# A gather kernel's expert loop: ScalarE's sums wait for the products themselves, coefficients and diagonals stand two half heads behind them

## The reference

```python
q = batchnorm(x @ w_q)                       # 2 x 8 heads of 128
sim = einsum('pbnhd,hkpd->pbnhk', q, keys)   # 2 x 8 x 128 scores a token
sx, ix = top_k(sim[0], 8); sy, iy = top_k(sim[1], 8)
scores, pk = top_k(sx[..., :, None] + sy[..., None, :], 8)
indices = take(ix * 128 + iy, pk)            # 8 heads x 8 experts a token
h = gelu(einsum('bnd,bnhkd->bnhk', x, down_embed[indices]))
h = softmax(scores) * h
out = einsum('bnhk,bnhkd->bnd', h, up_embed[indices])
return x + out
```

## Time and profile before

| | |
|---|---|
| median of 3 runs | 3230.07 us |
| lowest to highest | 3229.87 to 3230.78 us |
| the profiled execution, its own time | 3229.33 us |
| its span, first to last instruction | 3227.2 us |
| mean granted TensorE clock | 0.982 of full speed |
| gathered through GpSimd's queue | 1073.87 MB, 83.1% of 16 engines' span |
| HBM, read and written | 350 GB/s over the span |

### The profile page before, as it was taken

One profiled execution on the slowest core, in us unless ns is written; L12 is line 12 of the kernel. 1 busy time (PEld: TensorE's weight loads), 2 busy tenths in 40 slices (PEclk: granted clock), 3 DMA queues, 4 the chain that ended last, 5 costly groups with the idle time before them and its releaser, 6 DMA issues.

```text
span 3227.2 us, 36087 instructions
## 1 busy us (share of the span) xinstructions
PE 2857.5 (89%) x10310; PEld 1373.1 (43%) x10310; DVE 2407.8 (75%) x5220; ACT 1820.0 (56%) x5589; POOL 2141.3 (66%) x2224
## 2 busy tenths in 40 slices
PE   8999999898888888888888888889888888888877
PEld 6777767343333333333333333333333333333322
DVE  5888715887777777777777777777777777777765
ACT  3566502665565555655656555555656555655554
POOL 1555513777777777777777777777777777777773
PEclk9999999999999999999999999999999999999999
DMA  6222103999999999999999999999999999999996
GB/s 226 80 70 75 39 30 141 395 412 411 413 412 411 412 412 412 411 412 412 412 411 413 412 412 412 412 411 411 412 409 408 411 411 410 411 408 406 409 410 246
DMA packets 324861, 1133.07 MB, mean 351 GB/s; under 512 B 36331, under 2 KB 36971, under 8 KB 324024
## 3 DMA queue, kind: packets, MB, share of 16 engines
q0 software_dynamic: 294912, 1073.87, 83.1%
q1 hardware_dynamic: 29088, 56.41, 4.9%
q10 hardware_dynamic: 664, 0.50, 0.1%
HBM read 1113.87 MB, written 16.78 MB: 350 GB/s over the span
## 4 chain that ended last, share of the span: by engine, by line
DMA 40%; PE 16%; POOL 14%; issue 11%; DVE 4%; ACT 0%; POOLq 0%; ACTq 0%; DVEq 0%
DMA rows<-in_table,expert_idx 37%; POOL rows L785 13%; PE banks L1330 11%; PE banks L1309 3%; DMA expert_more_rows<-in_table,expert_idx 3%; POOL expert_more_rows L785 1%; PE banks L1244 1%; DVE expert_top_i L889 1%; DVE expert_diag L980 1%; DVE rows L966 0%; PE banks L1256 0%; DVE expert_top_s L881 0%; DVE expert_coef L972 0%; PE banks L1285 0%; DVE expert_best_i L912 0%
## 5 line engine op out<-in xcount | busy, mean ns | idle before, releaser
L785 POOL DMA_INDIRECT rows<-in_table,expert_idx x1824 | 1725.1, 946 | 658.0 <-issue 541.0
L1330 PE MATMUL banks<-rows,expert_diag 128*128 128x512 f32 x3648 | 1710.9, 614 | 307.3 <-DVE expert_diag L980 307.0
L1149 ACT ACTIVATE rows<-rows 128x512 f32<-128x512 f32 x1824 | 1124.3, 617 | 945.2 <-DVE expert_coef L972 942.8
L966 DVE TENSOR_TENSOR rows<-rows,banks 128x2048 f32<-128x2048 f32 x456 | 1043.0, 2287 | 543.0 <-DMA rows<-in_table,expert_idx 541.5
L1330 PEld LDWEIGHTS banks<-rows,expert_diag 128*128 128x128 f32 x3648 | 687.4, 194 | 1283.0 <-issue 752.8
L1309 PE MATMUL banks<-amat,expert_xnT 128*128 128x512 f32 x992 | 465.2, 592 | 2.0 <-ACT banks L1140 1.3
L980 DVE TENSOR_TENSOR expert_diag<-banks,expert_coef 128x512 f32<-128x512 f32 x512 | 348.2, 680 | 0.6
L1149 ACT ACTIVATION_READ_ACCUMULATOR rows<-rows 128x1 f32 x1824 | 339.9, 186 | 0.0
L1309 PEld LDWEIGHTS banks<-amat,expert_xnT 128*128 128x128 f32 x992 | 188.3, 190 | 238.8 <-issue 229.9
L785 POOL DMA_INDIRECT expert_more_rows<-in_table,expert_idx x224 | 212.7, 950 | 84.1 <-issue 73.9
L1330 PE MATMUL banks<-expert_more_rows,expert_diag 128*128 128x512 f32 x448 | 209.8, 612 | 39.1 <-DVE expert_diag L980 39.1
(11 more groups left out here) (125 smaller groups left out, 2087.8 us busy)
## 6 DMA issues: line engine op xcount, KB each, us to landing
rows<-in_table,expert_idx POOLq DMA_INDIRECT x1824, 14.6
attention_xT_t<-in_x_T SPq DMA_DIRECT2D x32, 256.0 KB, 3.1
attention_x_t<-in_x SPq DMA_DIRECT2D x32, 256.0 KB, 3.1
x_dram<-rows SPq DMA_DIRECT2D x32, 256.0 KB, 2.0
expert_x_t<-x_dram SPq DMA_DIRECT2D x32, 256.0 KB, 6.1
out_y<-expert_x_t SPq DMA_DIRECT2D x32, 256.0 KB, 6.1
rows<-in_w_q SPq DMA_DIRECT2D x4, 1024.0 KB, 6.1
rows<-in_w_qT SPq DMA_DIRECT2D x4, 1024.0 KB, 8.6
```

The costliest lines, as they stand in the source:

```text
L785: pool.indirect_dma_start(four(n)[:, k, :], None, table[:, :], bass.IndirectOffsetOnAxis(ap=idx[:, t % 2, at:at + 1], axis=0))\
L966: return dve.tensor_tensor(down, down, xn_ps[:, par, :].unsqueeze(1).to_broadcast([P, HALF, D]), ALU.mult)
L1149: ins = act.activation(down, down, ACT.Copy, accum_out=hid[:, j % RING, k:k + 1])
L1330: mm = pe.matmul(out_ps[:, par, :], diag[:, j % RING, k, :], four(t * HALVES + j)[:, k, D:2 * D], start=(j == 0 and k == 0), stop=(j == HA ...
```

## The change

VectorE now signals every `products` (`multiplied`), and ScalarE waits for that instead of for coefficients. The coefficients and diagonals in step j are those of half head j - 2 instead of j - 1; the two that are left over after the last tile stand behind the loop. TensorE's chunks 2 and 3 of the scores move from half heads 8 and 11 to 7 and 10, and the transposes from 14 to 13, since TensorE's matmuls now stand one VectorE step later. Chunks 0 and 1 stay. VectorE also waits, before the coefficients, for its own earlier products to be complete.

```diff
--- before.py
+++ after.py
@@ -992,15 +992,15 @@
                 for j in range(HALVES):
                     n = t * HALVES + j
                     dve.wait_ge(row_in[n % GROUPS], (n // GROUPS + 1) * 64)
-                    made_products = products(t, par, j)
-                    if first and j == 0:
-                        made_products.then_inc(ev["multiplied"], 1)
+                    products(t, par, j).then_inc(ev["multiplied"], 1)
+                    if n > 0:
+                        dve.wait_ge(ev["multiplied"], n)
                     if j in (4, 6, 11, 14) and more >= 2:
                         wait(dve, "scored", (t + 2) * NQ + (4, 6, 11, 14).index(j) + 1)
-                    if j > 0:
-                        coefficients(t, par, j - 1)
+                    if j > 1:
+                        coefficients(t, par, j - 2)
                     elif not first:
-                        coefficients(t - 1, 1 - par, HALVES - 1)
+                        coefficients(t - 1, 1 - par, HALVES - 2 + j)
                     if j == 0:
                         if more >= 1:
                             top_places(3)
@@ -1065,10 +1065,10 @@
                             weights(1 - par)
                         if more >= 2:
                             pair_places(0)
-                    if j > 0:
-                        diagonals(t, j - 1)
+                    if j > 1:
+                        diagonals(t, j - 2)
                     elif not first:
-                        diagonals(t - 1, HALVES - 1)
+                        diagonals(t - 1, HALVES - 2 + j)
 
             made = 0
 
@@ -1124,8 +1124,9 @@
             norm(2, 0, 1)
             wait(dve, "ident_kept", 1)
             run(step)
-            coefficients(NT - 1, 1, HALVES - 1)
-            diagonals(NT - 1, HALVES - 1)
+            for j in (HALVES - 2, HALVES - 1):
+                coefficients(NT - 1, 1, j)
+                diagonals(NT - 1, j)
             finish(NT - 1, 1, NT // 2 - 1)
 
         @block.scalar
@@ -1151,11 +1152,7 @@
 
             def step(t, par, half, more, first):
                 for j in range(HALVES):
-
-                    if first and j == 0:
-                        wait(act, "multiplied", 1)
-                    else:
-                        wait(act, "coef_done", t * HALVES + j)
+                    act.wait_ge(ev["multiplied"], t * HALVES + j + 1)
                     sums_of_products(t, j)
                     wait(act, "summed", t * HALVES + j + 1)
                     act.activation(act_h[:, j % RING, :], hid[:, j % RING, :], ACT.Gelu_apprx_tanh)\
@@ -1313,9 +1310,9 @@
                     mm.then_inc(ev["scored"], 1)
 
             def step(t, par, half, more, first):
-                chunk_at = {0: 0, 2: 1, 8: 2, 11: 3}
+                chunk_at = {0: 0, 2: 1, 7: 2, 10: 3}
                 for j in range(HALVES):
-                    if j == 14 and more >= 3:
+                    if j == 13 and more >= 3:
                         turn(t + 3)
                     if more >= 2:
                         for c in range(2):
```

## The result

The changed kernel takes 3237.14 us, the median of 14 runs (3235.16 to 3239.44), against 3230.06 us of 14 runs of the kernel before (3228.81 to 3232.06). The ratio is 1.0022, with a 95% interval of 1.0014 to 1.003: **7.1 us more, 0.22%**. The forecast was 3234.6 us, 4.5 us more, in a range of 3231.0 to 3238.5. The profiled execution took 3237.47 us.

The account below looks back on a forecast made before the run. The prediction took the DMA engines' gathers to bound the kernel. 1.1 us at the start plus 3.4 us at the end, 4.5 us on a median of 3230.07, gave 3234.6 us, in a range of 3231.0 to 3238.5.

Parts of the forecast that it names:

- The bound: Expert loop: DMA gathers set the pace, 5.09 us a half head; ScalarE's 945 us of idle time counted 0.
- Rival C: ScalarE's wait was a bound after all: 0.16 us off each half head, 3148 us, or a smaller part; chance 0.03.
- Coefficients and diagonals one step later in the middle: Middle of loop: slots freed some 5.1 us later, gathers' lead falls from 27.5 to about 22.4 us, cost 0.
- Rival B: Lead of 22.4 us too short for the DMA engines: each of 57 ring turns loses 1 us, 3287 us; chance 0.03.
- The prediction's own sign against itself: Middle of loop: DMA windows below 409 GB/s would mean the lead or the order of the scores matters after all.
- The added wait: VectorE's wait for its own products each half head: hidden in 1.2 us of idle time, counted 0.
- The start: Start of loop: first diagonals 1.6 us later, TensorE's first group partly at slow clock; 1.1 us, ends 0.5 and 2.9.
- two ways in which the clock could come back: TensorE's first group: as long after the first matmul as before, term 1.6 us; or at the same moment, 0.5 us.
- The end: After the last products: three groups of TensorE matmuls follow instead of two, last addition 3.43 us later.
- Scores half a head sooner: TensorE's score chunks and transposes: later steps in the first tile may be late, slots not; 0, at most 1.7 us.
- rival A: Start: slow clock through the first group and beyond, term from 3.0 up to 8 us, time 3238 us; chance 0.16.
- both terms and no other: Only the losses at loop start and end: 3233.5 to 3236.5 us, chance 0.68.

Follow-up runs that it names:

- e4_act: The kernel before, with only ScalarE's sums changed to wait for the products instead of the coefficients: 3230.96 us, ratio 1.0001.
- f2_nowait: The changed kernel without VectorE's added wait for its own products: 3234.16 us, ratio 1.0015 to the kernel before.
- e5_ring8: The kernel before with a ring of eight half heads for the gathers instead of nine: 3253.46 us, ratio 1.0073.
- f1_selfwait: e4_act plus VectorE's added wait for its own products, lag and score order as in the kernel before: 3232.11 us, ratio 1.0009.
- e1_tail: The changed kernel with coefficients and diagonals again one half head behind in the last tile: 3233.86 us, ratio 1.0011 to the kernel before.
- e2_start: The changed kernel with one half head of lag and the old score and transpose places in the first tile: 3237.11 us, ratio 1.0017 to the kernel before.
- e3_both: The changed kernel with one half head of lag in first and last tile, old score places in the first: 3232.69 us, ratio 1.0009 to the kernel before.
- g1_lean: The kernel before with VectorE's waits for up_done and scored moved to instructions without other waits, 609 instructions fewer: 3225.68 us, ratio 0.9989.
- g5_pairs: g1_lean with coefficients and diagonals made for two half heads at once from the second tile on: 3228.84 us, ratio 0.9994 to the kernel before.
- e7_warm: The changed kernel with seven extra TensorE matmuls while it waits for the first diagonals: 3234.84 us, ratio 1.0015 to the kernel before.

## Why the prediction was right or wrong

**The bound: right.** The gathers bound the loop before and after; ScalarE's 945 us of idle time were no bound, and e4_act shows the edit that gives the change its name at 0 within 1 us. Rival C is out.

**Coefficients and diagonals one step later in the middle, counted 0: right.** The lead fell to 23 to 24 us (forecast 22.4), and f2_nowait, with that lead, has the middle pieces of the kernel before. Rival B is out. Its trial by e5_ring8 changed more than the lead and proves nothing. The prediction's own sign against itself, a DMA window under 409 GB/s, did come up: 408 from 2000 to 2400 us. It was a false alarm. f1_selfwait has 411 GB/s in that window at the long lead and yet the same middle piece (2343.80 and 2343.58 us), and from 2800 to 3200 us the order is turned round, 402 GB/s in the kernel before and 409 in the changed one. The windows count what all DMA engines move, the pace is set by what lands last. The rows are f1_selfwait, then the kernel before, then the changed one:

```profile
2000.00:2400.00 400.00, 347.46 (x781) 146.08 (x780) 308.19 (x682) 236.64 (x724) 288.31 (x305) 0.98 1.03 411
```

```profile
2800.00:3200.00 400.00, 332.24 (x732) 135.95 (x730) 291.35 (x561) 231.57 (x720) 281.43 (x299) 0.98 1.01 402
```

```profile
2800.00:3200.00 400.00, 327.70 (x726) 133.36 (x724) 291.70 (x571) 231.48 (x720) 288.07 (x306) 0.99 1.02 409
```

GpSimd's waits for TensorE, which should have risen, are 86.5 us and not 84.3, so hardly:

```profile
  issue: 600.4, 1820
  PE banks L1327: 86.5, 109
```

That was a poor sign to name: once the ring is full, GpSimd waits as much at a lead of 24 us as at one of 28.

**The added wait, counted 0: wrong, and this is the step that failed.** I reasoned that VectorE has 1.2 us of idle time a half head to hide it, which is so, and looked only at VectorE's own time. The price lies elsewhere: it makes 390 instructions, all VectorE's, and each 128th instruction of VectorE comes with a fetch after which the gathers land 0.9 us late. f1_selfwait and f2_nowait put the wait at 1.2 to 3.0 us by their medians, and three long gaps more are 2.8. It is nearly all of the difference between 4.5 and 7.1 us.

**The start, taken at 1.1 us with ends of 0.5 and 2.9: the later first group was right, the clock's return was not as assumed, and the size is within the ends.** The profiled execution showed nearly the upper one: its first group had almost all passes at 1.2 GHz, 6.60 us. From the first products to the first release of a slot it is 15.60 us in the changed kernel, 14.27 in e1_tail and 14.76 in f2_nowait; with the old lag at the start it is 13.04, 13.98, 13.15, 14.16 and 13.42 us in before, e4_act, f1_selfwait, e2_start and e3_both. The means are 14.9 and 13.6, a term of 1.3 us; with g1_lean and g5_pairs (14.0 us each, old lag too) it is 1.2. Three executions against seven, each scattered by about 1 us, do not fix it better than that. The prediction had two ways in which the clock could come back, and neither holds: over these ten traces it returns 3.2 to 5.9 us after the start of the first group, and 11.3 to 14.9 us after the first products. The rule from the Trainium skill, "TensorE: Matmul & The Clock Gate", Part 1, that the moment of the clock's return does not follow the work, agrees with this scatter of about 1 us between kernels that are the same up to there. The prediction read it as a moment that stands, which would have made the term 0.5 us; the mean of the traces is nearer to the 1.6 of the shift alone. The clock's part can be had back: e7_warm gained 2.3 us.

**The end, 3.43 us: right,** to the hundredth in the trace, 3.3 us in the medians of e1_tail.

**Scores half a head sooner, counted 0: right.** VectorE waited in the first tile for chunk 0, which now comes a step later, 2.80 us ahead of the coefficients at 585.52 us, but no slot was late by it: half heads 9 to 21 are all issued 1.4 to 1.6 us later than before, by the clock of the span.

Of the rivals, A was forecast to decide beyond a first term of 3.0 us. That point was not passed in the mean (1.3 us); by its median the change is slower by over 0.2% for another reason, a third term that none of the rivals named. The sum as measured: 3.4 at the end, 1.3 at the start and 2.4 left for the instructions, 7.1 us; the 2.4 is what remains, and lies within the 1.2 to 3.0 us of the experiments.

**The range: right in part by luck.** To both terms and no other the forecast gave 3233.5 to 3236.5 us, and 3237.14 lies above that. It lies within 3231.0 to 3238.5 because the range was kept wide for rival A, a slow clock at the start; the room was filled by the fetched instructions.

## What to carry to other kernels

An idle engine's largest wait says nothing before it is known what the engine ahead of it waits for; here 945 us of it were worth nothing. When a kernel is bound by DMA, look for the moments at which the DMA engines run dry, at the start and the end of the loop, and price every edit there; in the middle look at what lands last, and whether long gaps come at a fixed count of some engine's instructions. Then the length of that engine's list has a price, waits included: a second wait ahead of an instruction was an instruction of its own here (f1_selfwait, 391 more), and moved to a neighbour that waited for nothing it was not (g1_lean, 609 fewer).

## What the runs showed of the hardware that was not expected

VectorE's instruction fetch makes gathers land late. Once in 128 of VectorE's instructions (127.8 to 128.0 in the mean of every trace looked at) the last of the 64 completions of a half head comes 0.9 us late, while the 60th does not. 100 instructions of VectorE more or less move the end by 0.5 to 0.8 us, in both directions. 450 fewer on GpSimd did not move the middle of the loop, and of the 8 KB packets that come at other counts of VectorE none lies in a long gap. Why VectorE's alone count stays open; that they go to the DMA engine that lands last would explain it, and is not shown.

A signal by two took the place of a wait: no VectorE instruction of g5_pairs that signals by two carries a wait, and 477 instructions that only wait are added.

Gathers into eight buffers, without the ninth that lies apart, moved 410 GB/s and not 412 from the start of the loop on, and 406 later, 15 us over the middle. The cause is open.
